# First batch projected straight into its strips, heads' outputs turned by VectorE and normalised by GpSimd, and a new table of offsets, in a two-layer transformer kernel

## Chip, cores and metric

The kernel runs on one core of a Trainium2 chip, as one launch. The metric is device microseconds of that launch. Everything is in f32.

## What is computed

Eight batches of 256 tokens of width 128 go through two post-norm layers; layer 1 takes layer 0's output.

```python
x = layernorm(x + attn0(x))  # 16 heads of 8, softmax(q k' / sqrt(8)), biases
x = layernorm(x + ffn0(x))   # 128->512, butterfly, gelu, butterfly, 512->128
x = layernorm(x + attn1(x))  # low-rank q and kv, rotary, causal, 4 kv heads
x = layernorm(x + ffn1(x))   # (silu(x wg) * (x wu)) wd, hidden 384, int weights
```

## The kernel before

**The unit of work.** A batch of one layer is a number b from 0 to 15 (layer 0 is b < 8, layer 1 the rest), and its 16 heads are heads 16b to 16b+15 of 256. All engines walk the same steps g = -34, -32, ... (`STEPS`), two heads a step. What stands in step g is set by hand: a piece of work with offset `AT_x` runs for batch b at g = 16b + `AT_x` (`batch_at`), and one that covers a tile of two batches at g = 32n + offset (`tile_at`). The table of offsets at the head of the file is thus the order of all five engines. In the text a step's *slot* is g mod 16, from r0 to r14; eight slots are one batch's period.

**Scores.** Q and K of a batch lie in `QK`, a ring of four, each head's 8 rows at the start of a strip of 32 partitions; the four strips are four row groups of TensorE, and `GROUPS` of four heads stand side by side. Each head's scores are made twice. `max_scores` (L292) runs 14 heads ahead (`LEAD`) into the ring `SM` of three PSUM banks; VectorE takes each query's maximum out of it (L668 in layer 0; L676, two custom instructions with an accumulator read each, in layer 1). The maxima are turned by TensorE (`mt`, L348), copied by ScalarE (L542) and sent by a DMA (L246) into the 32nd row of each strip, against a row of ones. `exp_scores` (L311) then makes the shifted, transposed scores in the ring `ST` of three banks, and ScalarE takes the exponent (L535) into `E`. `scores(g)` interleaves both kinds. In layer 1 GpSimd zeroes the masked half of each diagonal block (L824).

**Between two blocks of scores** TensorE does the other work of the step. It has two PSUM banks `G` for that, dealt in turn by `claim`, which waits until the bank's last reader is done. The chain of a batch is: Q and K projection (L447) -> ScalarE copy -> DMAs into the strips (L231; in layer 1 a DMA swaps halves and GpSimd rotates, L832 to L834, first); V (L461); PV per half batch (L479, slots r12 and r4), where the values carry columns of ones, so that each head's sum of exponents comes along; copy to `O` by ScalarE (L597); four transposes `T` by TensorE (L355, slot r6); reciprocal of the sums and the product with it by VectorE (L684, L687); two transposes `ATT` by TensorE (L405, slot r8) and a copy by ScalarE (L555); projection (L415, slot r10); residual and statistics by VectorE (L747, L632, L635); normalisation by GpSimd (L773 to L780); transpose `XT` back (L422, slot r0) and ScalarE's copy. The feed-forward parts are UP0 (L365), GELU (L602, at offset 66), DN0 (L389, slots r6 and r8 of every second batch), LN0 (GpSimd) and XT0 (L428); in layer 1 UP1 in three chunks (L376), each with a tanh (L549) and two VectorE products (L708, L710), and DN1 (L398).

**The start.** ScalarE's and SyncE's queues load x and the weights; the first batch goes the common way (projection, ScalarE copy, four DMAs, two from each queue). At g = -34 TensorE multiplies zeros three times (L453, 128x512). While no exponent scores exist yet (14 heads), `filler` (L322) puts matmuls in their place. Other loads are issued one per step from g = -20 (`LATE`).

```python
AT_QK, AT_QKIN, AT_ROPE = -34, (-32, -24), -28
AT_MT, AT_V, AT_PV = (-6, 2), 0, (12, 20)
AT_T, AT_ATT, AT_PROJ, AT_LN, AT_XT = 22, 24, 26, 28, 32
AT_UP1, AT_DN1, AT_LN1 = (34, 38, 40), 46, 50
AT_UP0, AT_GELU, AT_DN0, AT_LN0, AT_XT0 = (50, 54, 56, 66), 66, (70, 72), 74, 80
```

## Time and profile before

| | |
|---|---|
| median of 3 runs | 377.0 us (376.42 to 378.9) |
| the profiled execution, its own time | 378.37 us |
| its span, first to last instruction | 376.6 us |
| mean granted TensorE clock | 0.97 |
| busy: PE, VectorE, ScalarE, GpSimd | 341.9, 238.1, 203.9, 170.8 us |

The span is what rows and sums go by; the 1.8 us around it are taken to stay. PE is TensorE's matmul part, PEld its weight loads, DVE VectorE, ACT ScalarE, POOL GpSimd, SP SyncE; a q behind a name is that engine's instruction queue. A matmul of f32 stands in the trace as two records. The end of a matmul is modelled and overlaps the next, so the length of a piece of TensorE work is read from its start to the start of what follows it.

### The profile page before, as it was taken

The page shows a single profiled execution, that of the slowest core. Times are in us where ns is not written, and L with a number is a line of the kernel's source. Part 1 is how long each engine was busy: PE and PEld are TensorE (multiplying, and loading weights), DVE is VectorE, ACT ScalarE, POOL GpSimd, SP SyncE. Part 2 cuts the span into 40 slices and gives each one's busy share as a digit, 9 for nine tenths or more (in the row PEclk, how much of TensorE's full clock was granted, in tenths as well). Part 3 has the DMA queues.
Part 4 walks back from the last instruction along what each step waited for, and adds up shares of the span by engine and source line. Part 5 has one row for each costly group of instructions (what it writes and reads, how often), then busy time and mean ns, then how long its engine had stood idle before and what let it go on. Part 6 is the DMA issues. An engine that isn't in the chain of part 4 may idle for free.

```text
span 376.6 us, 10486 instructions
## 1 busy us (share of the span) xinstructions
PE 341.9 (91%) x3912; PEld 239.6 (64%) x3912; DVE 238.1 (63%) x907; ACT 203.9 (54%) x439; POOL 170.8 (45%) x284
## 2 busy tenths in 40 slices
PE   3989999999989999899998899799899999999872
PEld 2557666665648556575567666488677777777652
DVE  3365566577758577376764738548597878883354
ACT  2015666665694656746574545834665565656310
POOL 7036964020202502346143766616958685453621
PEclk9998999999999999899998989969999999999998
DMA  4493150101010101101111001110111111000000
GB/s 146 63 293 58 35 138 3 30 3 30 3 30 2 31 3 31 29 3 30 30 31 28 21 13 30 30 28 4 44 32 44 31 44 30 18 3 17 2 15 29
DMA packets 9219, 14.04 MB, mean 37 GB/s; under 512 B 2001, under 2 KB 4945, under 8 KB 9041
## 3 DMA queue, kind: packets, MB, share of 16 engines
q1 hardware_dynamic: 8656, 13.11, 15.1%
q8 instruction: 31, 0.51, 0.6%
q10 hardware_dynamic: 512, 0.26, 0.4%
q14 instruction: 20, 0.16, 0.2%
HBM read 5.76 MB, written 1.05 MB: 18 GB/s over the span
## 4 chain that ended last, share of the span: by engine, by line
PE 79%; POOL 6%; DVE 5%; ACT 4%; issue 3%; DMA 2%; POOLq 0%; DVEq 0%; ACTq 0%
PE SM L292 27%; PE G L479 13%; PE ST L311 6%; PE G L389 5%; PE G L376 4%; PE G L365 4%; PE G L447 3%; PE G L348 3%; PE G L355 3%; PE G L398 2%; PE G L461 2%; POOL QK L815 2%; PE G L415 2%; DMA QK<-mt 2%; PE ST L453 1%
## 5 line engine op out<-in xcount | busy, mean ns | idle before, releaser
L535 ACT ACTIVATE E<-ST 128x512 f32<-128x512 f32 (+1 forms) x256 | 125.4, 541 | 89.0 <-PE ST L311 88.8
L311 PE MATMUL ST<-QK 32*128 32x256 f32 (+1 forms) x1024 | 138.5, 380 | 9.6 <-ACT E L535 8.0
L292 PE MATMUL SM<-QK 31*128 31x256 f32 (+1 forms) x1024 | 140.2, 379 | 0.8 <-DVE mx L668 0.7
L292 PEld LDWEIGHTS SM<-QK 31*128 31x128 f32 x1024 | 93.3, 186 | 40.5 <-DVE mx L668 13.2
L668 DVE TENSOR_REDUCE mx<-SM 128x2 f32<-128x512 f32 x128 | 82.2, 685 | 56.5 <-PE SM L292 56.3
L311 PEld LDWEIGHTS ST<-QK 32*128 32x128 f32 x1024 | 91.8, 187 | 14.1 <-ACT E L535 9.9
L676 DVE CUSTOM_DVE_ANT_0 masked_s<-SM,mask_sb 128x256 f32<-128x256 f32 (+1 forms) x256 | 75.7, 351 | 36.2 <-PE SM L292 35.9
L824 POOL TENSOR_SCALAR_AFFINE_SELECT E<-E 128x512 f32<-128x512 f32 x64 | 39.1, 634 | 43.5 <-ACT E L535 43.5
L479 PE MATMUL G<-E,V 128*32 128x256 f32 x992 | 53.6, 356 | 0.0
L479 PEld LDWEIGHTS G<-E,V 128*32 128x32 f32 x992 | 28.4, 109 | 20.3 <-issue 4.6
L777 POOL TENSOR_SCALAR nm_a<-mv_a 128x2 f32<-128x2 f32 x15 | 2.9, 193 | 62.7 <-DVE mv_a L635 62.7
L376 PE MATMUL G<-xt,wf 128*128 128x256 f32 x84 | 23.0, 400 | 0.1
L597 ACT ACTIVATE O<-G 128x256 f32<-128x256 f32 x31 | 11.9, 384 | 18.0 <-PE G L479 18.0
L676 DVE DVE_READ_ACCUMULATOR2_ANT mx<- 128x1 f32 x256 | 21.2, 83 | 0.0
L777 POOL TENSOR_SCALAR nm_f<-mv_f 128x4 f32<-128x4 f32 x4 | 0.8, 195 | 43.0 <-DVE mv_f L635 43.0
L389 PEld LDWEIGHTS G<-down,hid 128*128 128x128 f32 x128 | 17.8, 220 | 1.0 <-issue 0.7
L389 PE MATMUL G<-down,hid 128*128 128x128 f32 x128 | 18.3, 303 | 0.0
L376 PEld LDWEIGHTS G<-xt,wf 128*128 128x128 f32 x84 | 15.0, 197 | 3.1 <-ACT mt L542 0.9
L365 PE MATMUL G<-xt,wup 128*128 128x512 f32 x32 | 16.8, 606 | 0.0
L542 ACT ACTIVATE mt<-G 8x256 f32<-8x256 f32 x32 | 11.4, 357 | 7.1 <-PE G L348 7.1
L447 PE MATMUL G<-xt,wqk_sb 128*128 128x256 f32 x32 | 9.9, 434 | 4.7 <-DMA bqk_sb<-bqk 4.7
L832 POOL TENSOR_TENSOR ry<-ry,ropec_sb 128x512 f32<-128x512 f32 x8 | 10.2, 1279 | 8.3 <-issue 4.9
(135 smaller groups left out, 453.8 us busy)
## 6 DMA issues: line engine op xcount, KB each, us to landing
QK<-qk SPq DMA_DIRECT2D x62, 64.0 KB
rs<-ry SPq DMA_DIRECT2D x16, 128.0 KB, 2.3
xb<-x_nat SPq DMA_DIRECT2D x1, 1024.0 KB, 8.1
out<-ln_g SPq DMA_DIRECT2D x8, 128.0 KB, 2.0
xt<-x_t SPq DMA_DIRECT2D x1, 896.0 KB, 6.7
wi<-wi_all SPq DMA_DIRECT2D x1, 576.0 KB, 4.9
QK<-mt SPq DMA_DIRECT2D x32, 8.0 KB
fac<-fac_u SPq DMA_DIRECT2D x1, 508.0 KB, 4.6
```

The lines of the kernel that those rows point to most:

```text
L292: ins = nc.tensor.matmul(SM[m % S_RING][:, cols], q, QK[rows, b % QK_RING, r, 1, keys], start=True, stop=True)
L311: ins = nc.tensor.matmul(ST[m % S_RING][:, c * T:(c + 1) * T - q0], QK[rows, b % QK_RING, r, 1, c * P:(c + 1) * P], QK[rows, b % QK_RING, ...
L365: nc.tensor.matmul(bank[:, :], wup[:, c * P:(c + 1) * P], xt[:, n * FT:(n + 1) * FT], start=True, stop=True).then_inc(F0["up_ps"], 1)
L376: ins = nc.tensor.matmul(bank[:, s * T:(s + 1) * T], wf[:, s, c * P:(c + 1) * P], xt[:, i * T:(i + 1) * T], start=True, stop=True)
L389: ins = nc.tensor.matmul(bank[:, i * W:(i + 1) * W], hid0[:, c, s * P:(s + 1) * P], down[:, c, :], start=(c == 0), stop=(c == HC - 1))
L447: ins = nc.tensor.matmul(bank[:, s * T:(s + 1) * T], w[:, s, :], x, start=True, stop=True)
L479: ins = nc.tensor.matmul(bank[VCOL * j:VCOL * (j + 1), q0:T], values, E[:, (2 * n + e) % E_RING, j, k * T:(k + 1) * T - q0], start=(e == 0 ...
L535: act.activation(E[:, a % E_RING, j, 0:n], ST[m % S_RING][:, 0:n], ACT.Exp, scale=SCALE)\
L597: act.activation(O[:, b % 2, t, :], g_bank["pv", n][:, 0:T], ACT.Copy).then_inc(A["o_ready"], 1)
L668: ins = nc.vector.tensor_reduce(mx[:, n % 2, :, i], bank[:, :].rearrange("p (q k) -> p q k", q=QT), AX.X, ALU.max, negate=True)
L676: ins = nc.vector.tensor_tensor_reduce(out=masked_s[:, m % 2, lo:hi], in0=bank[:, lo:hi], in1=mask_sb[:, T + lo - hi:T], scale=-1.0, scala ...
L824: nc.gpsimd.affine_select(out=e, in_=e, pattern=[[0, 4], [1, P]], compare_op=ALU.is_ge, fill=0.0, base=0, channel_multiplier=-1).then_inc( ...
```

## The change

- **First batch.** Its Q and K weights come as `wfirst`, spread so that the projection of one group of four heads lands in the strips at once; ScalarE copies from PSUM into `QK` with the bias, whose K part also writes the row of ones. Four such projections stand at g = -40, -12, -8, -4 in place of one projection and four DMAs. Batch 1 and 2 are projected at g = -10 and 2 (`EARLY`).
- **Zeros.** The three 128x512 matmuls read a tile `idle` that VectorE clears, and stand ahead of everything. The fillers cover 8 heads instead of 14 (`FILL`).
- **Loads.** Nine loads that were issued one per step are issued at once at the start, x_nat and the rest from g = -2.
- **Heads' outputs.** ScalarE's copy to `O`, TensorE's `T` and `ATT`, VectorE's product and ScalarE's copy to `att` go. VectorE turns PV's result, 32x32 block by block, from PSUM into `turned` (twice per batch, at the end of slots r12 and r4), takes the reciprocals (r6), GpSimd multiplies (r6), VectorE turns the product into `att` (r8). The projection's weight rows are reordered to fit.
- **New deal.** Q and K of layer 1 move from r14 to r8 (three steps earlier), of layer 0 they stay in r14; V of layer 0 from r0 to r4 (even b) or r8 (odd b); the third UP1 chunk from r8 to r12; the third UP0 chunk from offset 56 to 64; the rotation on GpSimd from r4 to r14; layer 1's last normalisation from r2 to r8. On SyncE the maxima's DMA comes first in its step.

```diff
-AT_QK, AT_QKIN, AT_ROPE = -34, (-32, -24), -28
-AT_MT, AT_V, AT_PV = (-6, 2), 0, (12, 20)
-AT_UP1, AT_DN1, AT_LN1 = (34, 38, 40), 46, 50
+AT_QK, AT_QKIN, AT_ROPE = (-34, -40), -28, -34
+AT_MT, AT_V, AT_PV = (-6, 2), ((4, 8), (0, 0)), (12, 20)
+AT_UP1, AT_DN1, AT_LN1 = (34, 38, 44), 46, 56
...
+FIRST_AT, EARLY, FILL = (FIRST, -12, -8, -4), (None, -10, 2), 8
...
         @block.tensor
-                if (b := batch_at(g, AT_T)) is not None:
-                    bank = claim(("t", b), A["at_ready"], b + 1, g)
-                    pe.wait_ge(A["o_ready"], 2 * (b + 1))
-                    for q in range(QT):
-                        for t in range(2):
-                            ins = nc.tensor.transpose(bank[:, (2 * q + t) * P:(2 * q + t + 1) * P],
-                                                      O[:, b % 2, t, q * P:(q + 1) * P], id32[:, :])
...
-                if (b := batch_at(g, AT_ATT)) is not None:
-                    bank = claim(("att", b), A["att_ready"], b + 1, g)
-                    pe.wait_ge(A["at_ready"], b + 1)
-                    for q in range(QT):
-                        ins = nc.tensor.transpose(bank[:, q * P:(q + 1) * P], at[:, q, :], id32[:, :])
...
+            pe.wait_ge(idle_ready, 1)
+            for i in range(S_RING):
+                nc.tensor.matmul(ST[i][:, :], idle[:, 0:P], idle[:, :], start=True, stop=True)
...
+                for r in range(GROUPS):
+                    if g == FIRST_AT[r]:
+                        bank = claim(("first", r), first_out, 2 * (r + 1))
...
+                        for s in range(2):
+                            ins = nc.tensor.matmul(bank[:, s * T:(s + 1) * T], wfirst_sb[:, r, s, :], xt[:, 0:T], start=True, stop=True)
...
         @block.scalar
-                if (b := batch_at(g, AT_ATT)) is not None:
-                    act.wait_ge(A["att_ps"], b + 1)
-                    if b:
-                        act.wait_ge(A["proj_ps"], b)
-                    act.activation(att[:, :], g_bank["att", b][:, 0:T], ACT.Copy).then_inc(A["att_ready"], 1)
...
+                        for s in range(2):
+                            act.activation(QK[:, 0, r, s, :], g_bank["first", r][:, s * T:(s + 1) * T], ACT.Identity,
+                                           bias=bfirst_sb[:, r, s:s + 1]).then_inc(first_out, 1)
...
-                        if b == 0:
+                        if b == 1:
                             act.wait_ge(A["qk_out"], 2)
                             act.wait_ge(zeros_ready, 1)
-                            for j in range(2, STRIPS):
-                                act.dma_start(QK[STRIP * j:STRIP * j + ROWS, 0, :, :, :], qk[j:P:STRIPS, 0, :, :]).then_inc(qk_in[0], 16)
+                            for j in range(STRIPS):
+                                act.dma_start(QK[STRIP * j:STRIP * j + ROWS, 1, :, :, :], qk[j:P:STRIPS, 1, :, :]).then_inc(qk_in[1], 16)
...
-                    act.activation(O[:, b % 2, t, :], g_bank["pv", n][:, 0:T], ACT.Copy).then_inc(A["o_ready"], 1)
...
         @block.vector
+                if (b := batch_at(g, AT_NORM)) is not None:
+                    dve.wait_ge(A["turned"], 2 * (b + 1))
...
+                    found = turned[:, :, :].rearrange("p t (x c) -> p (t x) c", c=BLOCK)
+                    nc.vector.reciprocal(rec[:, :, :], found[:, :, 2 * D:2 * D + 2]).then_inc(A["rec_ready"], 1)
+                if (b := batch_at(g, AT_ATT)) is not None:
+                    dve.wait_ge(A["at_ready"], b + 1)
+                    if b:
+                        dve.wait_ge(A["proj_ps"], b)
+                    nc.vector.transpose(att[:, :].rearrange("p (x t c) -> p x t c", t=2, c=2 * D), at[:, :, :, :].rearrange("p t x c -> p x t c"))\
+                        .then_inc(A["att_ready"], 1)
...
+                if (n := half_at(g, AT_PV)) is not None:
+
+                    b, t = divmod(n, 2)
+                    dve.wait_ge(A["pv_ps"], n + 1)
+                    if b:
+                        dve.wait_ge(A["at_ready"], b)
+                    nc.vector.transpose(turned[:, t, :], g_bank["pv", n][:, 0:T]).then_inc(A["turned"], 1)
...
         @block.gpsimd
+                if (b := batch_at(g, AT_NORM)) is not None:
+                    pool.wait_ge(A["rec_ready"], b + 1)
+                    if b:
+                        pool.wait_ge(A["att_ready"], b)
+                    found = turned[:, :, :].rearrange("p t (x c) -> p (t x) c", c=BLOCK)
+                    nc.gpsimd.tensor_tensor(at[:, :, :, :].rearrange("p t x (e d) -> p (t x) e d", d=D),
+                                            found[:, :, 0:2 * D].rearrange("p x (e d) -> p x e d", d=D),
+                                            rec[:, :, :].unsqueeze(3).broadcast_to([P, 2 * T // BLOCK, 2, D]), ALU.mult)\
+                        .then_inc(A["at_ready"], 1)
```

**The order of TensorE at the start.** Before (L447 projects, L453 multiplies zeros, L292 makes the scores for the maxima, L322 fills):

```order
1 L447 MATMUL G<-xt,wqk_sb 128x256 x2
2 L453 MATMUL ST<-QK 128x512 x3
3 L447 MATMUL G<-xt,wqk_sb 128x256 x2
4 L292 MATMUL SM<-QK 128x256 x2
5 L322 MATMUL ST<-QK 128x256 x2
```

Of the change (L388 multiplies zeros, L402 projects a group of the first batch, L338 makes the scores for the maxima, L494 projects batch 1, L368 fills):

```order
1 L388 MATMUL ST<-idle 128x512 x3
2 L402 MATMUL G<-xt,wfirst_sb 128x256 x2
3 L338 MATMUL SM<-QK 128x256 x8
4 L402 MATMUL G<-xt,wfirst_sb 128x256 x2
5 L338 MATMUL SM<-QK 128x256 x4
6 L494 MATMUL G<-xt,wqk_sb 128x256 x2
7 L338 MATMUL SM<-QK 128x256 x2
8 L368 MATMUL ST<-QK 128x256 x2
9 L338 MATMUL SM<-QK 128x256 x2
10 L368 MATMUL ST<-QK 128x256 x2
11 L402 MATMUL G<-xt,wfirst_sb 128x256 x2
```

The zeros now wait for nothing that is loaded, the first heads wait for one group's projection only, and the other three projections and batch 1's stand between the first scores.

**The order of TensorE in layer 1, slots r6 and r8.** Before (L355 is `T`, L376 an UP1 chunk, L405 `ATT`; the scores are L292 and L311):

```order
620 L355 MATMUL G<-id,O 128x128 x4
621 L376 MATMUL G<-xt,wf 128x256 x2
622 L292 MATMUL SM<-QK 128x256 x2
623 L311 MATMUL ST<-QK 128x256 x2
624 L292 MATMUL SM<-QK 128x128 x2
625 L311 MATMUL ST<-QK 128x128 x2
626 L376 MATMUL G<-xt,wf 128x256 x2
627 L405 MATMUL G<-id,at 128x128 x2
```

Of the change (L431 is an UP1 chunk, L494 the Q and K projection; the scores are L338 and L357):

```order
591 L431 MATMUL G<-xt,wf 128x256 x2
592 L338 MATMUL SM<-QK 128x256 x2
593 L357 MATMUL ST<-QK 128x256 x2
594 L338 MATMUL SM<-QK 128x128 x2
595 L357 MATMUL ST<-QK 128x128 x2
596 L494 MATMUL G<-xt,wl 128x256 x2
```

Both kinds of transposes are gone; the third UP1 chunk has left r8 and stands in r12, and the projection of Q and K has come from r14 in its place.

**The order of VectorE behind the last scores.** Before (L684 and L687 normalise the last batch's heads, L708 and L710 are the two products of an UP1 chunk, L747 is the last batch's attention residual, L641 its normalisation, L730 batch 14's last residual):

```order
710 L684 RECIPROCAL rec<-ST 128x32
711 L687 TENSOR_TENSOR at<-ST,rec 128x256
712 L708 SCALAR_TENSOR_TENSOR gated<-th,G 128x256
713 L710 TENSOR_TENSOR hid<-G,gated 128x256
714 L708 SCALAR_TENSOR_TENSOR gated<-th,G 128x256
715 L710 TENSOR_TENSOR hid<-G,gated 128x256
716 L747 TENSOR_TENSOR r_a<-SM,xb 128x256
717 L632 BN_STATS stats_a<-r_a 128x6 x2
718 L635 BN_AGGR mv_a<-stats_a 128x2 x2
719 L641 TENSOR_SCALAR ln_a<-r_a,mv_a,rstd_a 128x128 x2
720 L730 TENSOR_TENSOR r_g<-SM,ln_a 128x256
```

Of the change (L722 reciprocal, L747 and L749 the products of a chunk, L727 the turn into `att`, L786 the residual, L680 the normalisation, L769 batch 14's residual):

```order
761 L722 RECIPROCAL rec<-turned 128x32
762 L747 SCALAR_TENSOR_TENSOR gated<-th,SM 128x256
763 L749 TENSOR_TENSOR hid<-SM,gated 128x256
764 L727 STREAM_TRANSPOSE att<-at 128x256
765 L786 TENSOR_TENSOR r_a<-ST,xb 128x256
766 L670 BN_STATS stats_a<-r_a 128x6 x2
767 L673 BN_AGGR mv_a<-stats_a 128x2 x2
768 L680 TENSOR_SCALAR ln_a<-r_a,mv_a,rstd_a 128x128 x2
769 L747 SCALAR_TENSOR_TENSOR gated<-th,ST 128x256
770 L749 TENSOR_TENSOR hid<-ST,gated 128x256
771 L769 TENSOR_TENSOR r_g<-ST,ln_a 128x256
```

Batch 14's third chunk has moved from ahead of the last batch's residual to behind its normalisation; DN1 of batch 14 needs that chunk, and on TensorE it stands ahead of the last batch's `XT`, as before.

## Rows read from the trace of the kernel before

**Rows 1.** The page: busy time, and granted clock in 40 slices.
```profile
PE 341.9 (91%) x3912; PEld 239.6 (64%) x3912; DVE 238.1 (63%) x907; ACT 203.9 (54%) x439; POOL 170.8 (45%) x284
...
PEclk9998999999999999899998989969999999999998
```

**Rows 2.** Stages: length, busy PE, PEld, DVE, ACT, POOL; clock, DMA share, GB/s.
```profile
0.00:30.53 30.53, 22.47 (x155) 13.69 (x155) 13.50 (x22) 5.50 (x12) 10.51 (x15) 0.99 0.58 162
30.53:85.16 54.63, 53.55 (x630) 35.26 (x629) 33.86 (x63) 35.08 (x76) 28.59 (x39) 0.98 0.20 43
85.16:128.85 43.69, 41.18 (x477) 26.60 (x476) 29.29 (x61) 28.81 (x56) 9.81 (x20) 1.00 0.09 17
128.85:174.14 45.29, 42.83 (x477) 27.77 (x476) 28.82 (x60) 27.82 (x52) 13.55 (x23) 0.96 0.12 23
174.14:213.84 39.70, 37.95 (x451) 25.98 (x451) 26.10 (x147) 23.72 (x47) 17.09 (x25) 0.96 0.12 22
213.84:267.38 53.54, 46.95 (x527) 35.48 (x527) 32.46 (x179) 28.30 (x60) 30.88 (x53) 0.90 0.13 27
267.38:336.42 69.04, 67.82 (x932) 52.43 (x931) 55.76 (x315) 40.96 (x103) 45.16 (x78) 1.00 0.14 30
285.44:303.49 18.05, 17.75 (x241) 13.70 (x240) 14.55 (x83) 10.79 (x28) 12.51 (x22) 1.00 0.19 40
336.42:376.60 40.18, 29.14 (x273) 22.35 (x272) 18.27 (x64) 13.68 (x35) 15.25 (x34) 0.97 0.04 14
```

**Rows 3.** Timeline of PE, layer 1: start, length, idle before.
```profile
290.65 0.66 PE L355 MATMUL G<-id,O 128*128 128x128 f32 x4
291.14 1.03 PE L376 MATMUL G<-xt,wf 128*128 128x256 f32 x4
...
293.93 0.38 PE L405 MATMUL G<-id,at 128*128 128x128 f32 x2
294.25 0.48 PE L292 MATMUL SM<-QK 31*128 31x256 f32 x2
```

**Rows 4.** Groups of instructions: count, busy us, mean ns of one, idle before.
```profile
L687 DVE TENSOR_TENSOR at<-G,rec 128x256 f32<-128x256 f32 x15 | 6.4, 424 | 0.5
L684 DVE RECIPROCAL rec<-G 128x32 f32<-128x32 f32 x15 | 5.3, 352 | 3.5 <-PE G L355 3.5
L697 DVE TENSOR_SCALAR hid<-G,bhid 128x512 f32<-128x512 f32 x16 | 12.0, 747 | 0.4 <-PE G L365 0.3
L853 POOL TENSOR_TENSOR xb<-ln_a,bcon_sb 128x256 f32<-128x256 f32 x8 | 5.9, 735 | 0.7
L832 POOL TENSOR_TENSOR ry<-ry,ropec_sb 128x512 f32<-128x512 f32 x8 | 10.2, 1279 | 8.3 <-issue 4.9 <-DMA rs<-ry 3.4
```

**Rows 5.** Timeline of the start: loads landed, zeros, scores without other work, wait for maxima.
```profile
4.70 2.04 PE L447 MATMUL G<-xt,wqk_sb 128*128 128x256 f32 x4 [4.70 <-DMA bqk_sb<-bqk]
...
7.90 5.18 PE L453 MATMUL ST<-QK 128*128 128x512 f32 x6 [1.15 <-POOL QK L815]
...
12.92 1.03 PE L447 MATMUL G<-xt,wqk_sb 128*128 128x256 f32 x4
...
28.24 0.48 PE L311 MATMUL ST<-QK 32*128 32x256 f32 x2 [1.64 <-DMA QK<-mt]
```

**Rows 6.** Timeline behind the last scores.
```profile
356.90 0.38 ACT L597 ACTIVATE O<-ST 128x256 f32<-128x256 f32 x1 [1.08 <-PE ST L479]
...
360.63 0.68 PE L415 MATMUL SM<-wout_sb,att 128*128 128x128 f32 x4 [0.62 <-ACT att L555]
361.27 1.58 PE L398 MATMUL SM<-wf,hid 128*128 128x128 f32 x12
364.42 0.41 PE L422 MATMUL ST<-id,ln_a 128*128 128x128 f32 x2 [1.58 <-DVE ln_a L641]
```

**Rows 7.** Two steps with nothing between their scores: VectorE's maxima, start to start.
```profile
16.66 1.29 DVE L668 TENSOR_REDUCE mx<-SM 128x2 f32<-128x512 f32 x2 [0.24 <-PE SM L292]
...
18.19 1.29 DVE L668 TENSOR_REDUCE mx<-SM 128x2 f32<-128x512 f32 x2 [0.24 <-PE SM L292]
```

207 lines of the change are left out of this document (118 added, 89 removed).

## Prediction

> **What bounds the kernel now.** First the page's busy times: TensorE works 341.9 of 376.6 us, the others 45 to 63% [rows 1]. So I looked next where TensorE is not busy, with the table of stages [rows 2]: it idles 8.1 us before 30.53, 6.6 in 213.84 to 267.38, 11.0 behind the last scores, and hardly anywhere else (1.2 of 69.04 us in layer 1's even stretch). There a batch takes 18.05 us, TensorE is busy 17.75 and VectorE 14.55 of them. TensorE is the bound, and work taken from it shortens the batch one for one until VectorE, the nearest rival, is late. The row of the granted clock dips in six slices [rows 1]; where TensorE is the bound that costs time too.
>
> What a step costs without other work matters for a new deal. Two such steps follow one another at 1.53 us, set by VectorE's maxima: 16.66 to 18.19 [rows 7]. The scores alone need 1.07 us of TensorE there (sixteen records, start to start), so an empty gap of layer 0 wastes 0.46.
>
> **The change part by part.**
>
> *Transposes of the heads' outputs.* Start to start, `T` costs 291.14 - 290.65 = 0.49 us and `ATT` 294.25 - 293.93 = 0.32 [rows 3], 0.81 a batch, 13.0 for 16. All of it is on the bound, except where a step waits for another chain anyway.
>
> *VectorE in exchange.* It loses the product (0.42) and a reciprocal from PSUM (0.35, taken again from SBUF), and gains three 32x32 transposes of 128x256. No row shows one. Below, nothing excludes a fast one of 0.25; above, the nearest row of twice the size from PSUM is 0.75 (L697). I take 0.42, the row of the same size from PSUM [rows 4]. Then 3 x 0.42 - 0.42 = +0.84 a batch: 14.55 becomes 15.4 of some 17.2 us. By slots of layer 1: eight masked maxima are about 1.15 a step, so VectorE needs 1.15 + 0.35 + 0.85 in r6, 1.15 + 0.42 in r8 and 1.15 + 1.15 (residual, statistics) in r10, 6.1 together, against TensorE's 1.83 + 1.83 + 1.67 = 5.3; the three score banks carry about one step of such debt, and r12 and r14 (3.26 and 2.40 of TensorE) pay it back. I charge 0.1 a batch. At 0.75 each VectorE has 16.4, and r4 to r10 need 8.5 against 7.6: the debt no longer fits, and 0.9 a batch comes on top.
>
> The Trainium skill bears on this: "VectorE: DVE Perf Modes", section "The three transpose paths", gives 311 ns for VectorE's transpose of 128x128 in bf16, and TensorE as the path for a full one. An estimate from that page for twice the columns is 0.6 us; by it the three would add 1.8 - 0.42 = 1.4 a batch instead of 0.84, still below the bound. No run here shows it.
>
> *GpSimd* gains one product, 0.735 [rows 4]: 12.5 becomes 13.3 of 17.2. VectorE's turn into `att` waits for it in r8; between stand a whole block of maxima and GpSimd's 0.74. It is hidden while GpSimd reaches it in time. If that cover goes, every maximum is queued behind the waiting VectorE. The rotation (three times 1.28 [rows 4]) now stands right ahead of the mask of r0, which PV in r4 waits for. Where the step r0 was itself late (tiles' ends, g = 144 and 176) TensorE reaches PV about 4.3 us after `ln_a`, the mask is done after 3.84 + 1.22 = 5.1: up to 0.8 us lost at each. The DMAs into the strips have six steps more than they need.
>
> *ScalarE* loses three copies of 0.38 a batch [rows 6] and is bound nowhere but around GELU; nothing gained.
>
> *The deal in layer 1.* Gaps stay filled: r8 gets Q and K, r12 the third UP1, r14 keeps DN1. So a full batch is 18.05 - 0.81 + 0.1 = 17.3, and the even stretch 267.38 to 336.42 with four gives -3.0.
>
> *The deal in layer 0.* In 85.16 to 128.85 two batches took 43.7. Off: two `T` and two `ATT`, 1.6; V of g = 68 now stands ahead of the wait for GELU and its tables, which hides 0.5 of it; V no longer waits for ScalarE's copy of x behind `XT`, 0.5. Such a pair costs 2.6 less in g = 50 to 80; in g = 82 to 112 Q and K of layer 1 leave r14 empty twice, +0.9, less what those two slots saved: -2.0.
>
> *30.53 to 85.16 (g = 2 to 48).* I priced each step with the same pieces: 50.4 for 54.6. The 4.2 are 1.6 of `T` and `ATT`, 0.7 of V's wait at g = 32, about 1.2 of a low clock behind the wait for the maxima, and 0.7 of small waits for GpSimd's preparation, which now has its loads early.
>
> *128.85 and on to 267.38 beyond g = 112.* Four times 0.81 = 3.2; at g = 144 the wait is for GpSimd's chain, so `ATT` before it brings nothing (+0.3); empty r14 at 126 and 158, +1.1; one of the two PV waits, +0.8 (at 148 TensorE is slow anyway: the granted clock of the stage is 0.90 [rows 2]); at 176 the moved UP1 chunk covers 0.7 of the wait. Net -1.7.
>
> *Start.* Before, loads land at 4.70, zeros run 7.90 to 13.08 behind GpSimd's memsets, and first scores come at 13.97 [rows 5]. Six records of 128x512 in 5.18 us are 0.86 each; the projection took 2.04 at 4.70 and 1.03 at 12.92: TensorE did the same work at half its rate until the zeros were over, although the granted clock is 1.00 there. Now the zeros wait for a small VectorE memset alone and run about 2.0 to 7.2, then group 0's projection (1.0 to 2.0) and two ScalarE copies (0.8): first scores at about 9.7, 4.3 earlier. Part is given back: three more projections of 1.06 and batch 1's stand between these scores, each followed by ScalarE copies for which the next step waits, and ScalarE issues batch 1's four DMAs, some 3 us, ahead of group 2's copies. Adding up, g = 0 comes near 26 as before, but its exponent scores need not wait until 28.24 for the DMA of the maxima [rows 5], since the loads are already done. Step 2 starts near 27.9 instead of 30.53: -2.6 (ends: 0, if that DMA is as slow as before, and -4.3).
>
> *Behind the last scores.* One `T` and `ATT` under exponent scores go, -0.8. The last PV ends at about 356.8, its projection starts at 360.63 [rows 6], behind `T`, two UP1 chunks and `ATT`. Now 0.42 + 0.35 + 0.74 + 0.42 and hand-overs of 0.1: about 359.2, -1.4. But batch 14's third chunk now waits on VectorE behind the last batch's normalisation: two products (0.85), then DN1 (1.58), and only then `XT`, which had started at 364.42 right behind `ln_a`: +2.2. Together 0.
>
> Sum: -2.6 - 4.2 - 2.6 - 2.0 - 1.7 - 3.0 + 0 = -16.1. Span 360.5, its own time 378.37 - 16.1 = 362.3; the runs' median lies 1.4 below the profiled execution: 360.9. I say 361.
>
> **Rivals.**
> - *VectorE becomes the bound in layer 1.* For it: 15.4 of 17.2 us with an unseen instruction. At 0.75 a transpose layer 1's eight batches lose 0.9 each, 361 + 7 = 368. Against: the row of equal size is 0.42.
> - *The start gives nothing.* The four small projections, each with a round trip through ScalarE, eat the 4.3 us, and the maxima's DMA is as late as before: 361 + 2.6, about 364.
> - *More than forecast.* The dips of the clock total about 20 us at half rate before 370 [rows 1]; each followed a wait of TensorE. If most waits shrink enough, up to 8 us more come off: 353.
> - *Slower.* VectorE stands at `att` for GpSimd, which has only begun the rotation: 3.84 + 0.74 less the one step (1.5) of slack is 3.1 for each of 8 batches, and in layer 0 the same behind LN0 (about 4.3 us, four times): 361 + 25 + 11 = 397. It decides as soon as GpSimd falls some four steps behind, so that r14's work is still running in r6. It has 13.3 of 17.2 us, so I hardly believe it.
>
> The Trainium skill has one rule that would push towards this: "SBUF — State Buffer" says that VectorE and GpSimd share a port pair as an exclusive lock when VectorE has two SBUF inputs or runs in a two-port mode. The new turn out of SBUF could be such a case; if each `att` waited for a running rotation product of up to 1.28, layer 1 would give back at most 10 us, about 370. The trace of before shows GpSimd's products at steady means beside VectorE's work, so I give that 3%.
>
> **How the numbers follow.** Forecast (356 to 366) 0.60; VectorE's bound 0.14; start 0.10; more than forecast 0.09; the port 0.03; slower 0.04. The range takes the forecast with the start's ends (0 and -4.3) and the transposes' price up to 0.75: 353 to 369. A measurement of this kernel tells about 1% from no change. Faster by over 1% (below 373.2) is all but the last rival and a tail of the second: 0.93; within 1% 0.04; slower 0.03.
>
> **What would show it.** The transposes' rows at 0.35 to 0.5; TensorE without waits for VectorE in the even stretch and 17.3 us a batch; first scores near 9.7 and the exponent scores of g = 0 unheld; `XT` of the last batch right behind DN1 instead of behind `ln_a`; PV at g = 148 and 180 waiting for GpSimd. I am wrong if the period in layer 1 stays near 18, if TensorE's waits for VectorE's `att` show, or if the first 31 us are as long as before.

## Result, and the profile after

The changed kernel took 382.14 us (median of four executions, 379.92 to 383.76), the kernel before beside it 377.95. The ratio is 1.009, 95% interval 1.0049 to 1.0132. The forecast was 361 and at least 353 to 369: it was wrong, in size and in sign. Six more executions of the same kernel later (`after_again`) had a median of 375.24 (371.56 to 386.42), ratio 0.989 [0.983, 0.995]. So the changed kernel is not one number: its ten executions lie up to 15 us apart, where all those of before beside the experiments lay between 376.0 and 382.7, and no run shows whether the chip or chance put the first four at 380 and above. Here and below a ratio leaves out the slow executions, those over 1.5% above the fastest of the same kernel in its series, while a median takes in all, so that the two can differ. What differs between the executions is in the second row here, the granted clock.

The page of the changed kernel: busy times, and the granted clock in 40 slices, to be read against [rows 1].

```profile
PE 344.6 (91%) x3804; PEld 238.0 (63%) x3804; DVE 251.2 (66%) x940; ACT 189.4 (50%) x397; POOL 178.1 (47%) x299
...
PEclk9599999999999999999997889979999999998989
```

TensorE has 108 matmul records fewer, and yet is busy 2.7 us longer. The second slice shows 5: TensorE ran at 1.2 GHz, the lower of the clock's two levels, for most of it. The stages, cut at the same steps g as in [rows 2], with the same columns (length, busy, then the granted clock as the third number from the right):

```profile
0.00:33.51 33.51, 25.67 (x134) 14.76 (x134) 13.42 (x23) 6.40 (x14) 18.54 (x28) 0.85 0.45 151
33.51:86.21 52.70, 52.28 (x622) 34.81 (x621) 36.06 (x68) 33.51 (x72) 20.08 (x27) 1.00 0.21 46
86.21:128.34 42.13, 40.55 (x466) 25.87 (x465) 31.11 (x66) 26.36 (x50) 11.07 (x22) 1.00 0.06 15
128.34:170.88 42.54, 40.65 (x465) 26.39 (x465) 30.44 (x65) 25.31 (x47) 15.15 (x26) 1.00 0.12 27
170.88:212.48 41.60, 39.14 (x444) 27.09 (x443) 26.96 (x145) 22.49 (x43) 17.22 (x26) 0.92 0.12 28
212.48:267.44 54.96, 48.34 (x522) 35.28 (x514) 34.80 (x188) 26.57 (x55) 32.64 (x53) 0.88 0.10 21
267.44:336.39 68.95, 67.17 (x908) 51.06 (x907) 58.93 (x323) 36.80 (x91) 46.98 (x85) 1.00 0.13 30
283.67:301.24 17.57, 17.57 (x236) 13.43 (x235) 15.31 (x84) 9.76 (x24) 12.99 (x23) 1.00 0.18 41
336.39:380.60 44.21, 30.81 (x261) 22.75 (x260) 19.47 (x67) 11.98 (x30) 16.42 (x36) 0.91 0.04 13
```

| stage | before | after | change | forecast | us at the low clock, before and after |
|---|---|---|---|---|---|
| start to g = 2 | 30.53 | 33.51 | +3.0 | -2.6 | 0.8, 10.2 |
| g = 2 to 48 | 54.63 | 52.70 | -1.9 | -4.2 | 2.6, 0 |
| g = 50 to 80 | 43.69 | 42.13 | -1.6 | -2.6 | 0, 0 |
| g = 82 to 112 | 45.29 | 42.54 | -2.8 | -2.0 | 3.4, 0 |
| g = 114 to 176 | 93.24 | 96.56 | +3.3 | -1.7 | 13.7, 20.5 |
| layer 1's even stretch | 69.04 | 68.95 | -0.1 | -3.0 | 0, 0 |
| behind the last scores (g = 240 on) | 40.18 | 44.21 | +4.0 | 0 | 2.2, 8.1 |

In these two profiled executions the low level holds for 22.7 us of before and 38.9 of the changed kernel. Where TensorE sets the pace, half of such a stretch is lost: at most 11.3 and 19.4, which would be 8 of the 20 us between measurement and forecast.

**Two sorts of time.** An execution's mean granted clock and its span go together: in 17 executions of before, run beside the first experiments, a straight line through them falls by 3.3 us per 0.01 of clock, and 17 on another chip give 3.9. Changed kernels whose clocks spread by 0.02 or more give 2.8 to 3.5, and all of them together 3.3. I use 3.3 below to compare kernels "at clock 0.97", which is an estimate from these spans. By it before has a span of 376.9 (376.9 to 377.3 on four chips) and the changed kernel 372.7. One kernel's executions scatter around the line with a standard deviation of 0.3 to 1.4, so a difference of under some 0.7 us between two kernels says little. So the work as dealt is 4.2 us shorter, and a mean clock of 0.948 in the four executions on record (0.961 in the six later ones) against 0.970 takes away 7 (3). The forecast of -16 fell twice: three quarters of the gain were not there, and in the four executions on record the clock took more than the rest.

**Start.** The timeline of TensorE in the changed kernel, against [rows 5]; the last column is the idle time before and what ended it:

```profile
1.50 5.49 PE L388 MATMUL ST<-idle 128*128 128x512 f32 x6 [1.50 <-DVE idle L676]
6.78 1.24 PE L402 MATMUL G<-xt,wfirst_sb 128*128 128x256 f32 x4
8.95 1.13 PE L338 MATMUL SM<-QK 31*128 31x256 f32 x10 [0.93 <-ACT QK L606]
10.86 2.07 PE L338 MATMUL SM<-QK 31*128 31x256 f32 x6 [0.78 <-DVE mx L704]
12.86 2.07 PE L402 MATMUL G<-xt,wfirst_sb 128*128 128x256 f32 x4
15.87 2.07 PE L338 MATMUL SM<-QK 31*128 31x256 f32 x8 [0.93 <-ACT QK L606]
17.87 2.07 PE L494 MATMUL G<-xt,wqk_sb 128*128 128x256 f32 x4
...
24.97 0.48 PE L338 MATMUL SM<-QK 31*128 31x256 f32 x2 [2.43 <-ACT QK L606]
```

First scores come at 8.95, a little ahead of the forecast (9.7). But a projection that takes 1.24 at 6.78 takes 2.07 at 12.86: the granted clock is 0.5 from 10.6 to 20.8. TensorE had waited 0.93 for ScalarE's copies, and stood in a second wait, 0.78 for the maxima, when it fell. And the wait of 2.43 us at 24.97 is this, on ScalarE:

```profile
19.98 0.84 ACT L616 ACTIVATE qk<-G,bqk_sb 128x256 f32<-128x256 f32 x2 [4.17 <-PE G L494]
20.85 3.19 ACTq L622 DMA_DIRECT2D QK<-qk  x4
24.08 0.84 ACT L606 ACTIVATE QK<-G,bfirst_sb 128x256 f32<-128x256 f32 x2 [3.26 <-issue]
```

ScalarE issues batch 1's four DMAs for 3.19 us, and the copies of group 2, for which the scores stand, are queued behind them.

**The new operations** (groups, against [rows 4]):

```profile
L801 DVE STREAM_TRANSPOSE turned<-G 128x256 f32<-128x256 f32 x31 | 13.9, 449 | 14.5 <-PE G L520 14.3
L727 DVE STREAM_TRANSPOSE att<-at 128x256 f32<-128x256 f32 x16 | 7.0, 437 | 0.0
L881 POOL TENSOR_TENSOR at<-turned,rec 128x256 f32<-128x256 f32 x16 | 10.0, 628 | 99.6 <-DVE rec L722 99.6
L520 PE MATMUL G<-E,V 128*32 128x256 f32 x992 | 54.6, 361 | 0.5 <-POOL E L874 0.5
```

The turns cost 0.449 us from PSUM and 0.437 from SBUF: my 0.42 was near. VectorE never waits for GpSimd ahead of `att` (idle 0.0).

**Tail**, against [rows 6]:

```profile
348.16 1.74 PE L431 MATMUL G<-xt,wf 128*128 128x256 f32 x4
...
356.56 1.51 PE L520 MATMUL SM<-E,V 128*32 128x256 f32 x32
358.13 0.45 DVE L801 STREAM_TRANSPOSE turned<-SM 128x256 f32<-128x256 f32 x1 [0.17 <-PE SM L520]
...
359.06 0.63 POOL L881 TENSOR_TENSOR at<-turned,rec 128x256 f32<-128x256 f32 x1 [3.65 <-DVE rec L722]
359.58 0.42 DVE L747 SCALAR_TENSOR_TENSOR gated<-th,SM 128x256 f32<-128x256 f32 x1 [0.61 <-ACT th L590]
360.04 0.42 DVE L749 TENSOR_TENSOR hid<-SM,gated 128x256 f32<-128x256 f32 x1
360.38 0.43 DVE L727 STREAM_TRANSPOSE att<-at 128x256 f32<-128x256 f32 x1
360.96 0.68 PE L464 MATMUL ST<-wout_sb,att 128*128 128x128 f32 x4 [1.83 <-DVE att L727]
...
365.54 2.83 PE L453 MATMUL ST<-wf,hid 128*128 128x128 f32 x12 [3.03 <-DVE hid L749]
368.16 0.63 PE L471 MATMUL G<-id,ln_a 128*128 128x128 f32 x2
```

The projection of the last batch starts at 360.96, not at 359.2. The larger part of this, 1.3, is there before: the last PV ends at 358.07 instead of 356.8, because batch 13's third UP1 chunk, which the deal put into r12, runs at the low clock (348.16, the clock is 0.5 from 348.5 to 351.9), and step g = 252 takes 4.98 us, where before it took 2.29. Another 0.7 is VectorE's two feed-forward products (359.58, 360.04), which are ahead of `att` in its queue. DN1 waits 3.03 us, and at the low clock takes 2.83 instead of 1.58; `XT` behind it comes 3.7 us later than before.

### The profile page after: what moved, and what is told of

Same layout as the page of the kernel before. It is cut to its first block, busy times and chain, and to the rows that moved or that the text cites. A ratio compares the mean times of both kernels' runs of the same rounds, so it can differ in the third digit from the quotient of the medians.

```text
span 380.6 us, 10260 instructions
## 1 busy us (share of the span) xinstructions
PE 344.6 (91%) x3804; PEld 238.0 (63%) x3804; DVE 251.2 (66%) x940; ACT 189.4 (50%) x397; POOL 178.1 (47%) x299
## 4 chain that ended last, share of the span: by engine, by line
PE 76%; POOL 7%; issue 5%; ACT 5%; DVE 5%; ACTq 1%; POOLq 0%; DVEq 0%
PE SM L338 26%; PE G L520 11%; PE ST L357 6%; PE G L444 5%; PE G L431 5%; PE G L494 3%; PE G L420 3%; PE G L411 2%; PE G L453 2%; PE G L502 2%; PE G L464 1%; PE ST L388 1%; POOL ln_f L830 1%; ACT L576 1%; ACT E L576 1%
## 5 line engine op out<-in xcount | busy, mean ns | idle before, releaser
L338 PE MATMUL SM<-QK 31*128 31x256 f32 (+1 forms) x1024 | 145.9, 384 | 9.4 <-ACT QK L606 5.2
L357 PE MATMUL ST<-QK 32*128 32x256 f32 (+1 forms) x1024 | 137.9, 379 | 7.3 <-ACT E L576 7.3
L338 PEld LDWEIGHTS SM<-QK 31*128 31x128 f32 x1024 | 97.0, 189 | 52.8 <-DVE mx L704 15.5
L357 PEld LDWEIGHTS ST<-QK 32*128 32x128 f32 x1024 | 92.1, 187 | 11.2 <-ACT E L576 9.4
L881 POOL TENSOR_TENSOR at<-turned,rec 128x256 f32<-128x256 f32 x16 | 10.0, 628 | 99.6 <-DVE rec L722 99.6
L520 PE MATMUL G<-E,V 128*32 128x256 f32 x992 | 54.6, 361 | 0.5 <-POOL E L874 0.5
L520 PEld LDWEIGHTS G<-E,V 128*32 128x32 f32 x992 | 29.0, 111 | 22.3 <-issue 7.5
L801 DVE STREAM_TRANSPOSE turned<-G 128x256 f32<-128x256 f32 x31 | 13.9, 449 | 14.5 <-PE G L520 14.3
L431 PE MATMUL G<-xt,wf 128*128 128x256 f32 x76 | 22.5, 421 | 0.7 <-ACT xt L595 0.6
L444 PE MATMUL G<-down,hid 128*128 128x128 f32 x128 | 19.6, 317 | 0.0
L420 PE MATMUL G<-xt,wup 128*128 128x512 f32 x32 | 17.9, 642 | 0.0
L431 PEld LDWEIGHTS G<-xt,wf 128*128 128x128 f32 x76 | 13.6, 199 | 4.7 <-ACT xt L595 0.9
L747 DVE SCALAR_TENSOR_TENSOR gated<-th,G 128x256 f32<-128x256 f32 x19 | 8.0, 420 | 10.8 <-ACT th L590 10.7
L830 POOL TENSOR_SCALAR ln_a<-r_a,nm_a,rstd_a 128x128 f32<-128x128 f32 x30 | 13.2, 447 | 1.6
L736 DVE TENSOR_SCALAR hid<-G,bhid 128x512 f32<-128x512 f32 x16 | 11.6, 724 | 1.9 <-PE G L420 1.7
```

What stands on the lines that cost most here:

```text
L338: ins = nc.tensor.matmul(SM[m % S_RING][:, cols], q, QK[rows, b % QK_RING, r, 1, keys], start=True, stop=True)
L357: ins = nc.tensor.matmul(ST[m % S_RING][:, c * T:(c + 1) * T - q0], QK[rows, b % QK_RING, r, 1, c * P:(c + 1) * P], QK[rows, b % QK_RING, ...
L420: nc.tensor.matmul(bank[:, :], wup[:, c * P:(c + 1) * P], xt[:, n * FT:(n + 1) * FT], start=True, stop=True).then_inc(F0["up_ps"], 1)
L431: ins = nc.tensor.matmul(bank[:, s * T:(s + 1) * T], wf[:, s, c * P:(c + 1) * P], xt[:, i * T:(i + 1) * T], start=True, stop=True)
L444: ins = nc.tensor.matmul(bank[:, i * W:(i + 1) * W], hid0[:, c, s * P:(s + 1) * P], down[:, c, :], start=(c == 0), stop=(c == HC - 1))
L520: ins = nc.tensor.matmul(bank[VCOL * j:VCOL * (j + 1), q0:T], values, E[:, (2 * n + e) % E_RING, j, k * T:(k + 1) * T - q0], start=(e == 0 ...
```

## The experiments

Fourteen kernels beside before, on four chips. Times are medians; "span at 0.97" is the mean over the executions of span and clock, brought to clock 0.97 by the slope above. "Low" is how long the granted clock was under 1 within the span of the profiled execution, for before in that of [rows 1].

| kernel | us | ratio to before, 95% | mean clock | span at 0.97 | low, us |
|---|---|---|---|---|---|
| before, 17 executions on each of two chips | 379.1, 378.9 | | 0.970 | 376.9 | 22.7 |
| changed kernel | 382.14 | 1.009 [1.005, 1.013] | 0.948 | 372.7 | 38.9 |
| after_again | 375.24 | 0.989 [0.983, 0.995] | 0.961 | 372.8 | 49.1 |
| chain | 371.27 | 0.982 [0.977, 0.986] | 0.970 | 369.6 | 15.7 |
| old_table | 372.60 | 0.985 [0.982, 0.989] | 0.965 | 369.1 | 26.3 |
| tail | 372.44 | 0.981 [0.976, 0.986] | 0.962 | 370.8 | 40.3 |
| fill14 | 382.58 | 0.997 [0.993, 1.002] | 0.950 | 373.2 | 42.4 |
| qk_r14 | 378.14 | 0.989 [0.982, 0.996] | 0.957 | 372.5 | 22.1 |
| up0_56 | 378.06 | 0.999 [0.995, 1.003] | 0.952 | 371.8 | 35.5 |
| start_sp | 368.90 | 0.976 [0.971, 0.981] | 0.971 | 367.5 | 19.1 |
| rec_cut | 371.85 | 0.986 [0.980, 0.991] | 0.968 | 370.1 | 22.5 |
| v_4_8 | 365.22 | 0.966 [0.962, 0.970] | 0.979 | 366.2 | 15.5 |
| deal_sp | 374.99 | 0.983 [0.976, 0.990] | see below | 371.7 | |
| att_cut (one execution) | 371.89 | | 0.965 | 368.6 | 25.8 |
| hold | 366.04 | 0.964 [0.957, 0.970] | 0.986 | 369.6 | 9.0 |
| hold2 | 362.54 | 0.954 [0.948, 0.959] | 0.988 | 365.9 | 9.1 |

**chain: the heads' outputs alone.** Kernel before, with only the turns by VectorE and the product by GpSimd; start and table as before.

```diff
 AT_QK, AT_QKIN, AT_ROPE = -34, (-32, -24), -28
-AT_T, AT_ATT, AT_PROJ, AT_LN, AT_XT = 22, 24, 26, 28, 32
+AT_NORM, AT_ATT, AT_PROJ, AT_LN, AT_XT = 22, 24, 26, 28, 32
...
```

> The kernel before with the heads' outputs alone changed (VectorE turns, GpSimd normalises); start and offsets as before. Theory 1 (the transposes' 13 us really leave the bound, and start, new deal and end lose them again): each T and ATT comes off a step that TensorE fills, less some 3 us at waits: span 376.6 - 10 = 366 to 368, ratio 0.972 to 0.978. Theory 2 (taking them from TensorE brings nothing, since VectorE and the waits behind it take their place): span 374 to 377, ratio 0.99 to 1.0. In layer 1's even stretch theory 1 says 17.2 to 17.3 us a batch, theory 2 18.0.

Measured 371.27, and 7.3 us less than before at equal clock. This part of the change is good, by two thirds of the 11 us (16 times 0.81 - 0.1) which I gave it. The gain is missing in layer 1: 68.21 us against 69.04 in the even stretch.

**old_table: the changed kernel with the old offsets.**

```diff
-AT_QK, AT_QKIN, AT_ROPE = (-34, -40), -28, -34
-AT_MT, AT_V, AT_PV = (-6, 2), ((4, 8), (0, 0)), (12, 20)
-AT_UP1, AT_DN1, AT_LN1 = (34, 38, 44), 46, 56
-AT_UP0, AT_GELU, AT_DN0, AT_LN0, AT_XT0 = (50, 54, 64, 66), 66, (70, 72), 74, 80
+AT_QK, AT_QKIN, AT_ROPE = (-34, -34), -24, -28
+AT_MT, AT_V, AT_PV = (-6, 2), ((0, 0), (0, 0)), (12, 20)
+AT_UP1, AT_DN1, AT_LN1 = (34, 38, 40), 46, 50
+AT_UP0, AT_GELU, AT_DN0, AT_LN0, AT_XT0 = (50, 54, 56, 66), 66, (70, 72), 74, 80
```

> The changed kernel with the old offsets (Q and K of layer 1 in r14, V in r0, third UP1 chunk in r8, third UP0 chunk at 56, rotation and last normalisation where they were); new start and new chain stay. Against the changed kernel it prices the deal, against the chain alone the start. If the deal loses (bank wait of V behind the third UP0 chunk, empty gaps, late third UP1 chunk at the end): span 371 to 374, 7 to 9 us below the changed kernel's 380.6; the rest above the chain alone, some 3 to 5, is the start. If the deal is neutral and the loss lies elsewhere (clock): 379 to 381.

372.60, at equal clock 369.1. Set beside chain, the new start is worth 0.5 us, no more than the scatter; set beside the changed kernel, the new deal costs 3.6.

**tail: the last two batches' third UP1 chunk back in r8.**

```diff
...
+    for offset, batches in ((AT_UP1[2], range(NB, BATCHES - 2)), (40, range(BATCHES - 2, BATCHES))):
...
```

> The changed kernel with the third UP1 chunk of the last two batches back at offset 40, so that DN1 of batch 14 does not wait behind the last normalisation. If that order is what makes the end long: XT of the last batch right behind ln_a, 3 us less with the clock's dip at DN1, span 377.5, ratio to the kernel before 1.000 to 1.003. If the end is long for the clock or the turns alone: no more than 0.5 us less.

From g = 240 on it takes 42.19 us instead of 44.21, and at equal clock the whole is 1.9 less; the expectation had 3. This single offset, wrong in the two batches that end the kernel, is half of what the deal costs. old_table, with all offsets old, takes 38.31 there. Most of the rest is step g = 252 with batch 13's chunk (4.98 us against 2.29) and the low clock, 9.6 us of which stand in this stage of tail and 2.4 in old_table's.

**fill14 and after_again.**

```diff
-FIRST_AT, EARLY, FILL = (FIRST, -12, -8, -4), (None, -10, 2), 8
+FIRST_AT, EARLY, FILL = (FIRST, -12, -8, -4), (None, -10, 2), 14
```

> The changed kernel with fillers for 14 heads instead of 8, so that TensorE has work between the first scores. If the start is slow because the clock falls in the thin work from 10 to 21 us (scores, projections at half rate): the dip goes or shrinks, g = 2 starts 3 us earlier, at about 30.5 instead of 33.5, ratio about 0.992 of the changed kernel. If it is slow for the round trips through ScalarE and the issues of batch 1's DMAs alone: g = 2 at 33 or later, no change of the time.

> The changed kernel once more, unaltered, beside the others on one chip: how its spans spread with the granted clock. In the runs so far the kernels' spans follow the mean granted clock by about 3.3 us per 0.01, within one kernel too. Theory clock (the change costs clock wherever it runs): mean clock 0.945 to 0.955 in most of six runs, spans 377 to 382. Theory chance (its first four runs met a low clock by chance): clocks as the kernel before's, 0.958 to 0.975, spans 370 to 376.

With more fillers g = 2 came at 31.50 instead of 33.51 in the profile, but the low stretches only came later (22.1 for 3.4 us, 28.9 for 6.8), and at equal clock nothing is gained. The 2 us can't be read as the fillers' either: in the repeat of the changed kernel, same program, g = 2 starts at 37.50. The repeat shows the spread: six executions at clocks of 0.936 to 0.980 with spans of 384.5 to 369.6. Of its theories neither holds for all six: two are nearer to "clock", four to "chance".

**qk_r14 and up0_56: two places of the deal undone.** The first puts layer 1's Q and K and the rotation back, the second the third UP0 chunk.

```diff
-AT_QK, AT_QKIN, AT_ROPE = (-34, -40), -28, -34
+AT_QK, AT_QKIN, AT_ROPE = (-34, -34), -24, -28
```

```diff
-AT_UP0, AT_GELU, AT_DN0, AT_LN0, AT_XT0 = (50, 54, 64, 66), 66, (70, 72), 74, 80
+AT_UP0, AT_GELU, AT_DN0, AT_LN0, AT_XT0 = (50, 54, 56, 66), 66, (70, 72), 74, 80
```

> The changed kernel with Q and K of layer 1 back in r14 (and the rotation in r4), the one edit that fills the empty gaps at g = 94, 110, 126, 142, 158. If the empty gaps ahead of the steps that wait make the thin stretches in which the clock falls: mean clock up by 0.01, span 4 to 6 us below the changed kernel's. If only their 1.1 us of empty steps counts: 1 us below.

> The changed kernel with the third UP0 chunk back at offset 56. In r0 with that chunk, V claims the chunk's PSUM bank and TensorE waits 0.63 us for VectorE's L736, four times or more; if that is a part of the deal's loss: 2 to 3 us below the changed kernel at equal clock. If not: no change.

At equal clock 0.2 us, which is nothing, and 0.9. In the changed kernel the third UP0 chunk stands in r0 of g = 128 and 160 together with `XT` and V, and V waits for its bank: 0.63 us at 190.20, released by VectorE's `hid`; the steps before are empty. These two steps take 4.30 and 4.45 us instead of 1.68, against 1.16 saved in each empty r14 ahead of them; with the chunk back at 56 they take 2.50 and 2.65, with Q and K back in r14 3.51. Both medians are ruled by the clock.

**start_sp: who issues the DMAs.** old_table with 14 fillers, and batch 1's four DMAs issued by SyncE.

```diff
-FIRST_AT, EARLY, FILL = (FIRST, -12, -8, -4), (None, -10, 2), 8
+FIRST_AT, EARLY, FILL = (FIRST, -12, -8, -4), (None, -10, 2), 14
...
-                if b is not None and b != 1:
+                if b is not None:
...
-                        if b == 1:
-                            act.wait_ge(A["qk_out"], 2)
-                            act.wait_ge(zeros_ready, 1)
-                            for j in range(STRIPS):
-                                act.dma_start(QK[STRIP * j:STRIP * j + ROWS, 1, :, :, :], qk[j:P:STRIPS, 1, :, :]).then_inc(qk_in[1], 16)
```

> The kernel of old_table (new chain, new start, old offsets) with batch 1's four DMAs issued by SyncE and fillers for 14 heads. Theory issue: in the profile of the changed kernel ScalarE issues those DMAs from 20.85 to 24.04 while group 2's copies wait, so g = 2 comes 2.5 to 3 us earlier than 31.59, at 28.5 to 29, and the time is 368 to 370. Theory clock: the dip at the start stays whatever issues them, g = 2 at 31 or later, 372 as before.

368.90: faster than both kernels. Step g = 2 starts at 27.71 (I had predicted 27.9 for the change), and its start has no low clock. The four profiles with this start (start_sp, v_4_8, hold, hold2) have g = 2 between 27.53 and 27.75, the seven in which ScalarE issues between 31.50 and 37.50. SyncE with 8 fillers was not run, so whether the fillers have a part isn't shown. This window of it answers to the first row of stages above:

```profile
0.00:27.71 27.71, 21.81 (x163) 13.16 (x163) 13.78 (x23) 6.85 (x15) 18.56 (x28) 1.00 0.55 183
```

**rec_cut and att_cut: what sets layer 1's period.** Both are chain with a VectorE instruction of layer 1 cut short, one in r6, one in r8, so layer 1 is computed with stale values.

```diff
-                    nc.vector.reciprocal(rec[:, :, :], found[:, :, 2 * D:2 * D + 2]).then_inc(A["rec_ready"], 1)
+                    n_rec = 1 if layer(b) == 1 else 2 * T // BLOCK
+                    nc.vector.reciprocal(rec[:, 0:n_rec, :], found[:, 0:n_rec, 2 * D:2 * D + 2]).then_inc(A["rec_ready"], 1)
```

```diff
+                    n_x = 1 if layer(b) == 1 else T // BLOCK
-                    nc.vector.transpose(att[:, :].rearrange("p (x t c) -> p x t c", t=2, c=2 * D), at[:, :, :, :].rearrange("p t x c -> p x t c"))\
+                    nc.vector.transpose(att[:, 0:2 * BLOCK * n_x // 2].rearrange("p (x t c) -> p x t c", t=2, c=2 * D), at[:, :, 0:n_x, :].rearrange("p t x c -> p x t c"))\
```

> Kernel chain (the kernel before with only the heads' outputs turned by VectorE) with layer 1's reciprocal cut from 32 to 2 elements a partition: the other normalisers keep layer 0's last values, so layer 1's output is not the reference's. It takes about 0.25 us of VectorE a batch and nothing from TensorE. In chain VectorE works without a pause for 8.3 of each 17.85 us of layer 1 (284.35 to 292.64) and TensorE's projection of the heads waits 0.44 us for it in r10. Theory A (in this stretch VectorE, not TensorE, sets the period): the period falls by about the time cut, 17.85 to 17.6, the wait in r10 from 0.44 to 0.2, and the stretch g=178 to 240 from 68.21 to about 67.2. Theory B (TensorE is the bound, the wait in r10 is recovered elsewhere): the stretch stays at 68.2.

> Kernel chain with layer 1's turn of the normalised heads (VectorE, att<-at) cut from 256 to 32 columns: the rest of att keeps layer 0's values, so layer 1's output is not the reference's. It takes about 0.35 us of VectorE a batch out of r8, as rec_cut took 0.2 out of r6. rec_cut changed nothing: the period stayed 17.85 and TensorE's wait in r10 0.44, and VectorE only stood for the tanh of r6 instead. In the trace TensorE's projection in r10 waits for the PSUM bank of the third UP1 chunk of r8, that is for the chain maxima, att, gated, hid on VectorE. Theory C (that one chain, and not VectorE's sum of work, sets r10): the wait in r10 falls from 0.44 to 0.1 to 0.2 and the stretch g=178 to 240 from 68.21 to about 67.1. Theory D (the chain goes through ScalarE's tanh, which ends at about the same time as att): the wait stays above 0.35 and the stretch at 68.0 to 68.2.

First what is to be explained. The timeline of VectorE in chain, r8 of the batch at g = 194 (each maximum is a custom instruction and an accumulator read; the third row is the first of four such pairs, the rest of which is left out):

```profile
285.84 0.42 DVE L685 SCALAR_TENSOR_TENSOR gated<-th,G 128x256 f32<-128x256 f32 x1
286.30 0.42 DVE L687 TENSOR_TENSOR hid<-G,gated 128x256 f32<-128x256 f32 x1
286.64 0.41 DVE L650 CUSTOM_DVE_ANT_0 masked_s<-SM,mask_sb 128x256 f32<-128x256 f32 x1
...
287.75 0.44 DVE L665 STREAM_TRANSPOSE att<-at 128x256 f32<-128x256 f32 x1
288.11 0.38 DVE L685 SCALAR_TENSOR_TENSOR gated<-th,G 128x256 f32<-128x256 f32 x1
288.52 0.42 DVE L687 TENSOR_TENSOR hid<-G,gated 128x256 f32<-128x256 f32 x1
```

and of TensorE in chain, then in att_cut:

```profile
286.18 1.13 PE L368 MATMUL G<-xt,wf 128*128 128x256 f32 x4
...
289.00 0.38 PE L401 MATMUL G<-wout_sb,att 128*128 128x128 f32 x1 [0.44 <-DVE hid L687]
```

```profile
289.57 1.13 PE L368 MATMUL G<-xt,wf 128*128 128x256 f32 x4
...
292.16 0.71 PE L401 MATMUL G<-wout_sb,att 128*128 128x128 f32 x4 [0.20 <-DVE hid L688]
```

The rows of `hid` in chain end at 288.94 and the projection starts at 289.00. It doesn't wait for `att`, which was turned 0.8 us earlier, but for its PSUM bank, which UP1's third chunk (286.18) had filled and `hid` reads last. Between the two stands VectorE's queue: gated, hid, four maxima, `att`, gated, hid, without a pause. The new turn was put right into it. Against before, steps r6 and r8 lost 0.39 and 0.21 us of TensorE, and r10 grew by 0.40, from 2.00 to 2.40: two thirds given back, 0.2 a batch left.

rec_cut took 0.19 us (0.35 to 0.16) from VectorE a little earlier, and the even stretch stayed at 68.22: VectorE then waited 0.22 for the tanh of r6, ahead of the queue. att_cut took 0.23 (0.44 to 0.21) out of the queue itself, and the stretch fell to 67.27, that is by 0.24 in r10 of each of its four batches. So it isn't VectorE's sum of work that sets the period (theories A and B of rec_cut: neither held as put; the measured time was B's), but one chain through it (theory C). The stretch in rec_cut, then in att_cut:

```profile
263.33:331.55 68.22, 66.47 (x908) 50.09 (x907) 57.64 (x323) 36.84 (x91) 47.49 (x82) 1.00 0.14 30
```

```profile
264.82:332.09 67.27, 66.47 (x907) 50.11 (x907) 57.41 (x323) 36.81 (x91) 47.48 (x82) 1.00 0.14 31
```

The changed kernel's deal takes the third UP1 chunk out of r8, and its full batch (g = 192 to 206) is at 17.57 against chain's 17.85 and before's 18.05: here the deal does what it is for, r10 takes 1.70 us and TensorE waits for nothing. But two of the even stretch's batches aren't full. From g = 208 on no Q and K are left to project, r8 is empty, VectorE gets no pause from TensorE's work there, and TensorE waits for its maxima in r10:

```profile
311.43 0.48 PE L338 MATMUL SM<-QK 31*128 31x256 f32 x1 [0.64 <-DVE mx L712]
```

That step takes 2.85 us. The chunk in r12 costs its 1.06 as everywhere. So the two batches take 17.58 and 17.57 us, where before took 17.19 and 17.42 and chain 16.98 and 17.21. That is why the even stretch as a whole gained 0.1 us and not 3.0.

**v_4_8: start_sp with layer 0's V in r4 and r8.**

```diff
-AT_MT, AT_V, AT_PV = (-6, 2), ((0, 0), (0, 0)), (12, 20)
+AT_MT, AT_V, AT_PV = (-6, 2), ((4, 8), (0, 0)), (12, 20)
```

> The best kernel so far (start_sp: new start with SyncE's DMAs and 14 fillers, old deal, new heads' outputs) with only layer 0's V moved from r0 to r4 and r8 as in the change. If V in r0 costs its wait for the copy of x behind XT (0.6 us each at g=32, 80 and 112), the median falls by 1.5 to 2, 368.9 to about 367; stage g=2 to 50 loses 0.6, 50 to 82 and 82 to 114 about 0.6 each. Rival: in r4 and r8 V costs its full 1.0 on TensorE where r0 hid part of it in VectorE's time of an empty step: no gain or up to 1 us longer.

365.22, 3.7 less; 1.3 of it at equal clock, the rest by fewer low stretches (two of start_sp's, at 108.5 and 152.9, are gone). The stages lose 0.95, 1.88 and 2.34, where 0.6 each was expected; the last two hold those two low stretches, 3.4 us long each, half of which is lost. g = 114 to 142 grows by 2.08, where a low stretch now stands.

**deal_sp: start_sp's start under the changed kernel's whole table.** Its edit against start_sp:

```diff
-AT_QK, AT_QKIN, AT_ROPE = (-34, -34), -24, -28
-AT_MT, AT_V, AT_PV = (-6, 2), ((0, 0), (0, 0)), (12, 20)
+AT_QK, AT_QKIN, AT_ROPE = (-34, -40), -28, -34
+AT_MT, AT_V, AT_PV = (-6, 2), ((4, 8), (0, 0)), (12, 20)
...
-AT_UP1, AT_DN1, AT_LN1 = (34, 38, 40), 46, 50
+AT_UP1, AT_DN1, AT_LN1 = (34, 38, 44), 46, 56
...
-AT_UP0, AT_GELU, AT_DN0, AT_LN0, AT_XT0 = (50, 54, 56, 66), 66, (70, 72), 74, 80
+AT_UP0, AT_GELU, AT_DN0, AT_LN0, AT_XT0 = (50, 54, 64, 66), 66, (70, 72), 74, 80
...
```

> The changed kernel with 14 fillers and SyncE issuing batch 1's DMAs: it differs from start_sp in the deal of work alone. At equal granted clock the deal costs 3 to 4 us (372 against 368.9). Theory A (the changed kernel's low mean clock comes from its start, where TensorE waits for ScalarE): with this start the mean granted clock is 0.965 or more and the median near 372. Theory B (it comes from the deal: thin gaps, an empty r8, a longer tail): the mean granted clock is near 0.955 and the median near 376.

One of its six executions, the profiled one, took 429 us at a granted clock of 0.75 nearly from end to end; it says nothing on the deal. The other five have clocks of 0.957 to 0.983, mean 0.970, and spans that come to 371.7 at 0.97. That is theory A's clock and its equal-clock time; the median, 374.99, lies between the theories. fill14 differs from deal_sp only in who issues batch 1's DMAs, and had a mean clock of 0.950 over twelve executions, on another chip. The profiles say the same: all seven with ScalarE issuing (the changed kernel, after_again, old_table, tail, fill14, qk_r14, up0_56) have a low stretch in the first 31 us; the four others with the new start (start_sp, v_4_8, hold, hold2) have none before 108 us. That the deal has a part in the spread isn't excluded.

**hold and hold2: TensorE kept at work in the waits.** v_4_8 with matmuls of the idle zeros ahead of long waits, into a bank that is overwritten next; hold2 leaves out the first two.

```diff
+KEEP, KEEP_LN = {70: 1, 102: 1, 134: 2, 166: 3}, {144: 3, 176: 1}
...
+            def keep(bank, n):
+                for _ in range(n):
+                    nc.tensor.matmul(bank[:, :], idle[:, 0:P], idle[:, :], start=True, stop=True)
...
+                    if m - 1 in KEEP:
+                        n = tile_at(m - 1, AT_DN0[0])
+                        held[n] = claim(("dn0", n, 0), F0["res_done"], 2 * n + 1)
+                        keep(held[n], KEEP[m - 1])
...
+                    keep(bank, KEEP_LN.get(g, 0))
                     pe.wait_ge(A["ln_ready"], b + 1)
```

> Kernel v_4_8 with TensorE kept at work in the long waits of layer 0: matmuls of the idle zeros (128x512, 0.85 us each) into a bank that is free and is overwritten next: 1, 1, 2 and 3 of them ahead of the wait for GELU in g=70, 102, 134 and 166 (waits 1.19, 1.19, 1.75, 2.56), 3 and 1 ahead of the wait for GpSimd's normalisation in g=144 and 176 (2.66, 1.32). The result is unchanged. In v_4_8 the granted clock falls to half right behind the waits of 1.75, 2.66 and 2.56 us, for 3.4, 3.4 and 6.8 us. Theory A (TensorE's idleness in the waits lowers the clock): these three stretches go, the mean granted clock rises from 0.979 to about 0.99, and half of their 13.7 us, 6.8, comes off: median 358.5. Theory B (the clock falls by itself or from load): the low stretches stay, and the median is 365 or, where a filler reaches past its wait, up to 1 us more.

hold2 against hold:

```diff
-KEEP, KEEP_LN = {70: 1, 102: 1, 134: 2, 166: 3}, {144: 3, 176: 1}
+KEEP, KEEP_LN = {134: 2, 166: 3}, {144: 3, 176: 1}
```

> Kernel hold without the fillers in g=70 and 102. In hold these two waited themselves for their bank, which ScalarE frees with the copy of V behind GELU (1.95 us), and took 1.8 us each instead of hiding; behind the first the clock fell at 109.5 for 6.8 us. The others hid: g=134 went from 6.92 to 5.38, 144 and 146 together from 8.69 to 7.08, 166 from 10.02 to 7.10, and no low clock followed them. Theory A (waits of TensorE lower the clock): the stretches at 191, 208 and 235 stay away, none comes at 109, mean granted clock 0.99, median 359 to 360. Theory B (a low stretch comes anyway, only elsewhere, as at 109.5 in hold): the mean granted clock stays near 0.98 and the median at 362 to 365.

One of the three waits in v_4_8 (g = 144), and one of the fillers in hold that had to wait itself (g = 70):

```profile
207.13 0.41 PE L471 MATMUL G<-id,ln_a 128*128 128x128 f32 x2 [2.62 <-POOL ln_a L825]
```

```profile
108.03 1.13 PE L328 MATMUL G<-idle 128*128 128x512 f32 x2 [1.95 <-ACT V L643]
```

Windows of v_4_8 over g = 134 to 142, 144 and 146, and 166 and 168:

```profile
187.65:203.57 15.92, 14.16 (x159) 11.71 (x155) 10.36 (x58) 7.37 (x15) 8.38 (x14) 0.89 0.09 19
203.57:212.25 8.68, 6.02 (x47) 4.13 (x46) 2.62 (x20) 3.95 (x9) 5.44 (x12) 0.80 0.13 30
231.81:245.69 13.88, 11.32 (x77) 9.59 (x73) 6.22 (x30) 6.08 (x10) 3.17 (x5) 0.75 0.10 19
```

the same steps in hold2:

```profile
189.28:203.66 14.38, 14.38 (x162) 10.75 (x158) 10.36 (x58) 7.36 (x15) 8.38 (x14) 1.00 0.10 21
203.66:210.76 7.10, 7.06 (x54) 4.06 (x53) 2.52 (x19) 3.84 (x9) 5.17 (x12) 1.00 0.16 37
230.32:241.13 10.81, 10.81 (x83) 8.01 (x79) 6.23 (x30) 6.08 (x10) 3.19 (x5) 1.00 0.13 25
```

In all three the waits end within 0.15 us of where they did in v_4_8, counted from the step's start (they are for GELU with its table loads, and for GpSimd's normalisation), the granted clock stays at its upper level, and 1.5, 1.6 and 3.1 us go. hold lost it again: its fillers in g = 70 and 102 had to wait for a bank themselves (1.95 us, behind ScalarE's copy of V), pushed those steps from 4.93 to 9.05 and 6.75 us, and a low stretch followed the first. In hold2 a low stretch followed g = 102, whose wait of 1.20 us is not filled, and one more than in v_4_8 lies in the tail; in v_4_8 the same waits were followed by none. hold2's expectation thus came half true: the three stretches stay away and the mean clock is 0.988 (theory A, which had 359 to 360 us), and one comes elsewhere, with a median of 362.54 (theory B, 362 to 365). So that the waits brought the low clock is shown for the three that were filled, in the profiles of both kernels, and the mean clocks over six executions each agree (0.986 and 0.988 against v_4_8's 0.979); low stretches still come elsewhere, behind waits that are open, and not behind each of them. hold2, at 362.54 us, is the fastest kernel here: 0.954 of before [0.948, 0.959].

## Why the prediction was wrong

- **"It shortens the batch one for one until VectorE is late."** This step failed, and with it the gain of chain in the even stretch: 0.2 a batch instead of 0.8 - 0.1. Steps r6 and r8 lost 0.60 and not 0.81, and 0.40 came back in r10. I had priced VectorE's sum of work in r6 to r10 and let "the three score banks" carry the debt. The sum isn't what is late. The trace of before already had the wait, 0.30 us in r10 of the four batches of the even stretch, and a stretch of 8.0 us (290.74 to 298.76) in which VectorE never pauses; in chain it is 8.3:

```profile
295.48 0.38 PE L348 MATMUL G<-id,mx 128*8 128x128 f32 x2 [0.30 <-DVE hid L710]
```

I had read busy shares of the batch and of slots, and not the row of who ends TensorE's idle time in r10. An engine at 80% can hold the bound at one place.
- **"Gaps stay filled ... and the even stretch 267.38 to 336.42 with four gives -3.0."** This step failed in the changed kernel itself, and it is the 2.9 us missing there. The full batch came near (17.57 against 17.3 forecast, 18.05 before). But I multiplied it by four: the part at g = 178 to 190 gained 0.1, the full batch 0.5, and the last two, which project no Q and K, lost 0.4 and 0.2 with an empty r8 and the third chunk in r12. "Hardly anywhere else" for TensorE's idle time misled too: by [rows 2] the stages from 30.53 to 213.84 hold 7.8 us of it.
- **Transposes**: 0.449 and 0.437 us against 0.42; right, and rival VectorE at 0.75 is out. My estimate of 0.6 for this size from the Trainium skill ("VectorE: DVE Perf Modes", "The three transpose paths") was too high; the measurement decides. The slots r6 to r10 add up to 6.2 and not 6.1, which changes nothing. The port rule of the Trainium skill's "SBUF — State Buffer" was not put to the test: in the trace no rotation product ran beside a turn into `att`. Beside a mask (0.29 us of it at 228.83) or small GpSimd products the turns took 433 to 441 ns, as they did alone.
- **Start**: first scores at 8.95 (9.7 forecast), exponent scores of g = 0 not held by the DMA, both right. "g = 0 comes near 26" failed, by two terms. ScalarE's DMA issues were priced (3 us) but taken as hidden beside work, while group 2's copies and TensorE stood 2.43 us behind them; and the clock, which I charged nowhere in the start, was at 1.2 GHz for 10.2 us, of which up to half is lost. start_sp, without both, has g = 2 at 27.71, so the -2.6 holds for a start that this change isn't.
- **Deal**: I summed slots of full batches. Where it has its cover it pays (17.57 in the full batch, V in r4 and r8 1.3 us at equal clock). What I missed: the third UP1 chunk of the last two batches falls behind the last scores, 1.9; V with `XT` and UP0 in one r0 behind an empty r14, about 0.9. With V's gain the rest of the deal costs nearly 5 us at equal clock, of which these experiments assign 3; 0.7 more is the even stretch (68.95 against old_table's 68.22), and the remainder stays open. Right was the PV wait for GpSimd at g = 180 (0.49 us, L520 above) but not at 148, and "empty r14".
- **Tail**: the last projection at 360.96 instead of 359.2. The first step that failed is "the last PV ends at about 356.8": it ended at 358.07, behind batch 13's chunk in r12 at the low clock. The second is 0.42 + 0.35 + 0.74 + 0.42 with nothing between: two products of the feed-forward chunk stand there in VectorE's queue. Then came DN1 at the low clock (1.3 more); the order that I charged with +2.2 cost 1.9 (tail).
- **Clock**: I had it as the rival "more than forecast", with the waits shrinking and 8 us more to win, and gave its opposite no chance. The start and the tail got more and longer waits instead, and 38.9 us of the profiled execution were at the low level, against 22.7. This term I had put at nothing; the sign of the result hangs on it alone: at equal clock the change is 4.2 us faster.

The rival for slower, VectorE standing for GpSimd's rotation ahead of `att`, did not occur. So the outcome "slower" came by a way that stood in none of the cases; the upper end of the range, 369, took in no loss by the clock, although before's own row shows six dips [rows 1].

What stays open: whether the deal, apart from the start, makes the clock less steady (five executions of deal_sp are too few); what part of the low stretches between 198 and 257 in the kernels with ScalarE issuing goes with the deal; and why the same wait is followed by a low stretch in one kernel and not in another.

## What to carry to other kernels

Ask of each idle row of the bounding engine what releases it, and follow that releaser's queue backwards: work that is moved to an engine with time to spare costs its full length if it lands in that queue, and here cost nothing 2 us earlier. Price the batches at the ends apart from the full ones: a gap that fills itself in the middle is empty there. A DMA issue is work of the engine that issues it; where a critical copy stands behind it, give it to an idle queue. And where TensorE has a long wait on the path that sets the end, put a matmul that nobody reads into the wait, provided that its bank is free: here it gave back up to 3 us behind a wait of 2.6, and cost 1.8 where the bank was not free.

## What the hardware did that I had not expected

- The same kernel's executions differ by the granted clock: 0.936 to 0.980 for the changed kernel with spans of 384.5 to 369.6, but 0.978 to 0.982 with spans of 362.3 to 363.5 for v_4_8. Fewer low stretches don't make a kernel steady, though: hold2, with the highest mean, ran at 0.977 to 0.996 (362.9 to 357.0).
- Low stretches follow waits that are short beside them: waits of 1.75, 2.62 and 2.56 us in v_4_8 were followed by 3.4, 3.4 and 6.8 us at 1.2 GHz. The Trainium skill ("TensorE: Matmul & The Clock Gate", "Why this matters for your kernels") asks for TensorE to be kept from idling between matmuls; hold2 agrees, with the numbers above, and shows that matmuls of zeros serve. The waits here are shorter than the gaps that the page warns of; the measurement decides.
- One execution of deal_sp ran 396 of its 427 us at a granted clock of 0.75, neither of the two levels, on one core alone. The other five did not.
